# Segment attention on one core: where the same-segment products, the own values and the choice stand in the order of a step

## The chip, the cores and the metric

The kernel runs on one core of a Trainium2 chip. Each core has TensorE (PE in the rows, its weight loads PEld), VectorE (DVE), ScalarE (ACT), GpSimd (POOL), SyncE for DMAs (SP), a 128-partition SBUF and eight PSUM banks of 512 float32 columns per partition. The engines run their own instruction queues in order and wait for each other by semaphores. The metric is the time of one execution on the device in microseconds, as a median over runs; all data are float32 unless a row says otherwise.

## The reference, cut to what matters

Five layers, each added to the running activations `x` (32 x 32 tokens of 256 features): an attention with distance bias over a context, an attention over the 32 tokens of a batch, a quantised feed-forward layer, an attention over the context without heads, then the segment attention that the change touches, and a layer of experts. The segment attention is, with the layer norm of `x` as its input (16 heads of 16 features):

```python
long_out = _mha(x, lt_w_in, lt_b_in, lt_w_out, lt_b_out, H)
seg = jnp.argmax(x @ protos.T, axis=-1)
same = seg[:, :, None] == seg[:, None, :]
short_out = _mha(x, st_w_in, st_b_in, st_w_out, st_b_out, H, mask=same)
cnt = jnp.sum(jax.nn.one_hot(seg, NSEG, dtype=jnp.int32), axis=1)
tok_cnt = jnp.take_along_axis(cnt, seg, axis=1)
short_out = jnp.where((tok_cnt == 1)[..., None], x, short_out)
combined = jnp.concatenate([long_out, short_out], axis=-1)
return combined @ fus_w.T + fus_b
```

A token that is alone in its segment keeps its own features in place of the short output. `_mha` projects to queries, keys and values, takes the softmax of the scaled scores (with -1e9 where the mask is off) and weighs the values. The experts' layer routes each token to two of eight experts.

## The kernel before, in words

The 1024 tokens are eight tiles `t` of 128 tokens, each of four batches of 32. The segment attention (class `SegmentAttention`) works in steps `u = 2t + s`: an even step (`s = 0`) is the long attention of tile `t`, an odd step (`s = 1`) the short one. The steps are a pipeline written out by hand: in one step each engine does pieces of several tiles, in a fixed order, by the functions `pe_step`, `act_step`, `pool_step` and `dve_step`. Steps -3 to -1 run at the end of the stage before, 0 to 8 in a block of their own, 9 to 14 together with the first work of the experts' layer (`experts`), whose own order for the end of the last tiles follows the loop.

In step `u` PE does, in this order: in an odd step the transposes of the normalised tokens of tile t + 2 (`turn_tokens`) and of the one-hot segment of tile t + 1 (L2122), in an even step the segment logits of tile t + 1 (L2127); queries and keys of step u + 2 (`project_qk`, L859); the scores of step u + 1 (`per_batch`, L899), and at once the projection of its own values (`project_tokens`, L868); in an odd step the same-segment products of tile t + 1 (L2139), four of 8 x 32 by 8 x 32 which give 1 where two tokens of a batch share a segment; the weighing of the values of step u (`weigh_values`, L926); then in an even step the short output of tile t - 1 (`last_y`, L2169 and L2174), in an odd step the fused output of tile t - 1 (`fused_near` and `fused_far`, L2181 and L2187).

ACT copies what PE leaves: transposed tokens (L2062) and one-hot (L2065), keys (L2073) and queries (L2078) with their bias, the own values (L2028), the attention sums and each head's own part of the weighed values (L2033, L2036), then the exponent of step u + 1 (L2043), and in an even step the short output of tile t - 1 (L2049). POOL spreads the keys over heads (L875) and the values over batches (L882), adds a bias row (L2018) and takes the root for the normalisation (L1993).

DVE does in step `u`: `features` of step u - 1 (reciprocal of the sums, L2208, product, L2209, and a transpose of 32 x 32 blocks, L959), the transpose of the probabilities of step u (L936), in an even step the argmax of tile t + 1 (L2220 to L2227) and statistics of tile t + 3 (L2193 to L2196), in an odd step the normalisation of tile t + 3 (L2202), then `off_maximum` of step u + 1: in an odd step the maximum of the long scores and its subtraction (L2239, L2240), in an even step the mask, the maximum and the subtraction for the short ones (L2246, L2250, L2251). In an odd step follows the mask's making: a copy of the same-segment products out of PSUM (L2302), the mask (L2304) and the count of others in the segment (L2305, L2306). Last come, in an even step, the choice between short output and own features of tile t - 1 (`short`, L2262), in an odd step the add of the fused output to `x` (L2268).

One PSUM bank, `v_bank`, holds in turn the logits, the transposed one-hot, the own values and the same-segment products. Their uses are numbered in `v_use`; `vb_full` counts what PE has filled, `vb_done` what has been read, and PE waits before each use for the one before it to be read. The scores stand in banks 2 and 3, 256 columns in each; the columns behind are not used. PE raises `s_full` when the scores of a step are there, and DVE raises `s_read` when it has read them. `same_ready` tells that the mask is made, `short_ready` that the choice of a tile is done; PE's fused output and its next short output wait for it.

Of the kernel before, what the change touches and what calls it, by code (L numbers as in the profile page):

```python
# [25 lines left out]
NB, SQ, D, SK = 32, 32, 256, 257  # L26
NH, DH = 16, 16
P = 128
# [948 lines left out]
def there(u, count=NT):  # L977
    return not isinstance(u, int) or 0 <= u < count
# [944 lines left out]
class SegmentAttention:  # L1923


    def __init__(self, nc, in_wn, in_shared, sem, psum, bank, c, x, w, loaded):
# [29 lines left out]
        x_part, fused = f_bank[:, D:2 * D], f_bank[:, 0:D]  # L1956
        v_part, same_part = v_bank[:, 0:D], v_bank[:, D:D + SQ]
        logits, hot_part = v_bank[:, D + SQ:D + SQ + NE], v_bank[0:NE, D + SQ + NE:D + SQ + NE + P]
        y_part, others_part = y_bank[:, 0:D], y_bank[:, D:D + P]
# [7 lines left out]
        y_full, y_ready, short_ready = sem("y_full"), sem("y_ready"), sem("short_ready")  # L1967
        hot_ready, same_ready = sem("hot_ready"), sem("same_ready")
        qk_full, k_ready, q_ready, kbd_ready = sem("qk_full"), sem("k_ready"), sem("q_ready"), sem("kbd_ready")
# [6 lines left out]
        for u in range(-3, U + 2):  # L1976
# [7 lines left out]
            if there(u + 1, U):  # L1984
                v_use["v", u + 1] = len(v_use) + 1
            if s == 1 and there(t + 1):
                v_use["same", t + 1] = len(v_use) + 1
        self.ahead = in_shared.at
# [123 lines left out]
        def pe_step(pe, u):  # L2112
# [21 lines left out]
            if there(u + 1, U):  # L2134
                scores(pe, u + 1)
            if s == 1 and there(t + 1):
                pe.wait_ge(vb_done, v_use["same", t + 1] - 1)
                for b in range(BT):
                    ins = nc.tensor.matmul(same_part[SQ * b:SQ * b + SQ, :], hotT[:, SQ * b:SQ * b + SQ],  # L2139
                                           hotT[:, SQ * b:SQ * b + SQ], start=True, stop=True,  # L2140
                                           skip_group_check=True)
                ins.then_inc(vb_full, 1)
            if there(u, U):
                values(pe, u)
            if s == 0 and there(t - 1):
                last_y(pe, t - 1)
# [5 lines left out]
        def scores(pe, n):  # L2152
            pe.wait_ge(kbd_ready, n + 1)
            pe.wait_ge(q_ready, n + 1)
            at_least(pe, s_read, n)
            per_batch(nc, s_banks, tokens(qT[n % 2]), heads_apart(kbd[n % 2]), 0, True).then_inc(s_full, 1)
            at_least(pe, vb_done, v_use["v", n] - 1)
            project_tokens(nc, v_part, xT[:, n // 2], w[kinds[n % 2] + "_qkv"][:, :, 2 * D:3 * D]) \
                .then_inc(vb_full, 1)
# [69 lines left out]
        def off_maximum(dve, n):  # L2229
# [7 lines left out]
            at_least(dve, p_ready, n - 1)  # L2237
            if n % 2 == 0:
                st.link(dve, nc.vector.tensor_reduce(by_bank, banks, AX.X, ALU.max))  # L2239
                nc.vector.tensor_tensor(here[:].rearrange(in_banks_of, f=2), banks,  # L2240
# [43 lines left out]
        def dve_step(dve, u):  # L2284
# [3 lines left out]
            if there(u, U):  # L2288
                turn(dve, u)
            if s == 0 and there(t + 1):  # L2290
                argmax(dve, t + 1)
# [6 lines left out]
            if s == 1 and there(t + 1):  # L2298
                n = t + 1
                dve.wait_ge(vb_full, v_use["same", n])  # L2300
                at_least(dve, y_full, n - 2)
                nc.vector.tensor_copy(same[:], same_part).then_inc(vb_done, 1)  # L2302
                dve.wait_ge(vb_done, v_use["same", n])
                st.done(nc.vector.tensor_scalar(shut[:], same[:], 1.0, 1e9, ALU.subtract, ALU.mult))  # L2304
# [4 lines left out]
                dve.sem_inc(same_ready, 1)  # L2309
            if s == 0 and there(t - 1):  # L2310
                short(dve, t - 1)
            if s == 1 and there(t - 1):
# [656 lines left out]
```

## Time and profile before

| what | value |
|---|---|
| median of 3 runs | 713.54 us (711.33 to 713.84) |
| profiled execution | 710.97 us, its span 709.2 us |
| PE busy | 626.6 us, 88% of the span |
| DVE busy | 459.7 us, 65% |
| ACT busy | 368.5 us, 52% |
| POOL busy | 314.7 us, 44% |
| mean granted clock of PE | 0.95 |

The span runs from the first instruction to the last; the profiled execution's own time is 1.8 us longer. The segment attention's loop lies between 459 and 563 us of it. A busy share is an average over stages with different limits, so the shares above say little about one stage; the busy time by stretch and the timeline of one pair of steps do. In a row of a timeline, the bracket at the end is the time for which the engine sat idle before the instruction, and what released it. Matmul records come two to a float32 matmul; their ends are modelled.

### The profile page before, as it was taken

How to read it: one execution, taken by the hardware profiler on the slowest of the kernel's cores; microseconds unless marked ns; L12 is line 12 of the kernel's file. 1: busy time of each engine (PE TensorE's matmuls, PEld its weight loads, DVE VectorE, ACT ScalarE, POOL GpSimd, SP SyncE). 2: the span in 40 equal slices, each digit the busy share in tenths (PEclk: the TensorE clock that was granted, in tenths of full speed). 3: DMA queues.
4: the chain of work that ended last, by engine and by line, in shares of the span. 5: the costliest groups of instructions: out<-in, count | busy, mean ns of one | idle time of the engine just before them, and what ended most of it. 6: DMA issues, size and time to landing. Idle time of an engine off the chain costs nothing.

```text
span 709.2 us, 18761 instructions
## 1 busy us (share of the span) xinstructions
PE 626.6 (88%) x7075; PEld 476.2 (67%) x7075; DVE 459.7 (65%) x1279; ACT 368.5 (52%) x992; POOL 314.7 (44%) x458
## 2 busy tenths in 40 slices
PE   4999999999999999779957999889998859999990
PEld 3788888888877787544445876668777645777760
DVE  1797777776686988843988735487888873333320
ACT  1656665656566897653956434356656521322220
POOL 1346666666653897300000302166655413655641
PEclk9999999999999999879977999999999978999995
DMA  8733333333300000291003347093020031444434
GB/s 276 260 100 91 83 73 89 88 87 74 86 2 4 3 4 4 96 352 59 0 0 144 120 158 293 2 394 128 3 68 2 2 114 45 63 66 68 62 39 73
DMA packets 31704, 65.20 MB, mean 92 GB/s; under 512 B 5792, under 2 KB 21792, under 8 KB 29312
## 3 DMA queue, kind: packets, MB, share of 16 engines
q1 hardware_dynamic: 26016, 55.73, 23.8%
q0 software_dynamic: 4688, 7.18, 6.4%
q8 instruction: 58, 0.95, 0.5%
q10 hardware_dynamic: 912, 1.10, 0.5%
q14 instruction: 30, 0.25, 0.1%
HBM read 57.67 MB, written 7.37 MB: 92 GB/s over the span
## 4 chain that ended last, share of the span: by engine, by line
PE 64%; DVE 21%; ACT 5%; issue 4%; DMA 2%; SPq 2%; POOL 1%; DVEq 0%; ACTq 0%; POOLq 0%
PE psum L2647 8%; PE psum L491 7%; PE psum L499 7%; PE psum L2657 4%; PE psum L529 4%; PE psum L1502 3%; PE psum L1479 3%; PE psum L859 3%; DVE ff_peak L1520 2%; PE psum L515 2%; PE psum L544 2%; PE psum L851 2%; PE psum L868 2%; PE psum L899 2%; DMA wn<-in_w_down 2%
## 5 line engine op out<-in xcount | busy, mean ns | idle before, releaser
L802 POOL TENSOR_SCALAR bias<-dist,cst 128x257 f32<-128x257 f32 x128 | 61.4, 499 | 74.1 <-issue 42.8
L491 PE MATMUL psum<-ctxT,shared 128*128 128x257 f32 x256 | 65.9, 401 | 2.3 <-DMA msk<-in_mask 2.2
L424 ACT ACTIVATE prob<-s_sb,negm 128x257 f32<-128x257 f32 x128 | 64.9, 509 | 1.4 <-DVE negm L665 1.3
L499 PE MATMUL psum<-shared,ctxT 128*128 128x256 f32 x256 | 60.6, 379 | 0.0
L661 DVE CUSTOM_DVE_ANT_0 s_sb<-psum,bias 128x257 f32<-128x257 f32 x128 | 46.6, 420 | 19.8 <-PE psum L515 17.2
L2647 PE MATMUL psum<-ex_w,shared 128*128 x184 | 58.3, 460 | 0.6 <-ACT shared L2540 0.6
L1741 POOL TENSOR_TENSOR wn<-wn,cst 128x1 f32<-128x1 f32 x8 | 4.7, 590 | 120.8 <-DVE wn L1868 120.8
L491 PEld LDWEIGHTS psum<-ctxT,shared 128*128 128x128 f32 x256 | 47.1, 194 | 12.6 <-issue 4.9
L413 ACT COPY kT<-psum 128x257 f32<-128x257 f32 x64 | 24.0, 375 | 60.3 <-PE psum L491 60.3
L499 PEld LDWEIGHTS psum<-shared,ctxT 128*128 128x128 f32 x256 | 46.2, 190 | 5.0
L2830 DVE TENSOR_TENSOR shared<-psum,shared 128x352 f32<-128x352 f32 x23 | 12.1, 525 | 48.6 <-ACT shared L2556 48.6
L2647 PEld LDWEIGHTS psum<-ex_w,shared 128*128 128x128 f32 x184 | 33.1, 190 | 15.4 <-issue 0.8
L1479 PE MATMUL psum<-shared,ff_used_up 128*128 128x512 f32 x96 | 41.6, 593 | 0.0
L875 POOL TENSOR_TENSOR shared<-shared,cst 128x512 f32<-128x512 f32 x32 | 35.1, 1117 | 7.7 <-ACT shared L2073 6.8
L2556 ACT ACTIVATE shared<-psum 128x352 f32<-128x352 f32 x23 | 10.7, 464 | 52.8 <-PE psum L2647 52.8
L2657 PE MATMUL psum<-ex_w,shared 128*128 x138 | 33.7, 380 | 0.8 <-DVE shared L2821 0.8
L681 DVE COPY pT<-psum 128x512 f32<-128x512 f32 x32 | 22.1, 691 | 17.9 <-PE psum L529 16.1
L529 PE MATMUL psum<-cst,prob 128*128 128x128 f32 x256 | 33.2, 273 | 0.2 <-DVE mx L661 0.2
L1479 PEld LDWEIGHTS psum<-shared,ff_used_up 128*128 128x128 f32 x96 | 18.1, 191 | 22.0 <-issue 21.5
L859 PE MATMUL psum<-shared,late 128*128 128x128 f32 x256 | 32.9, 283 | 0.0
L1520 DVE TENSOR_REDUCE ff_peak<-shared 128x1 f32<-128x512 f32 (+1 forms) x24 | 22.8, 952 | 14.6 <-ACT shared L1373 14.2
L529 PEld LDWEIGHTS psum<-cst,prob 128*128 128x128 f32 x256 | 29.5, 141 | 2.9 <-issue 0.4
(357 smaller groups left out, 1614.6 us busy)
## 6 DMA issues: line engine op xcount, KB each, us to landing
ctxT<-in_ctx_T SPq DMA_DIRECT2D x32, 257.0 KB
ex_w<-in_w SPq DMA_DIRECT2D x1, 5632.0 KB, 18.2
kpos<-in_kpos SPq DMA_DIRECT2D x32, 128.5 KB
msk<-in_mask SPq DMA_DIRECT2D x32, 128.5 KB
near_turned<-in_ctx_T_tiles SPq DMA_DIRECT2D x4, 1028.0 KB
ff_used_up<-in_ctx_T_tiles SPq DMA_DIRECT2D x4, 1028.0 KB
near_rows<-in_ctx_tiles SPq DMA_DIRECT2D x4, 1024.0 KB, 7.4
ff_used_up<-in_ctx_tiles SPq DMA_DIRECT2D x4, 1024.0 KB, 6.6
```

The costliest lines, as they stand in the source:

```text
L424: nc.scalar.activation(prob[n % 2][:, g, :], s_sb[n % 2][:, g, :], ACT.Exp, bias=negm[:, b, g:g + 1], accum_out=esum[t % 2][:, b, g:g + 1]) \
L491: ins = nc.tensor.matmul(kv[m][:, 0:SK], w["xa_k"][:, k, P * m:P * m + P], ctxT[n % BT][:, k, :], start=(k == 0), stop=(k == KT - 1))
L499: ins = nc.tensor.matmul(kv[0][:, D * i:D * i + D], ctxT[n % BT][:, k, P * i:P * i + P], w["xa_v"][:, k, :], start=(i == 0 and k == 0), st ...
L529: ins = nc.tensor.transpose(pt[j][:, at:at + P], prob[n % 2][:, g, P * i:P * i + P], c.ident)
L661: nc.vector.tensor_tensor_reduce(s_sb[n % 2][:, g, :], sc[g][:, 0:SK], bias[n % 2][:, g, :], 1.0, float("-inf"), ALU.add, ALU.max, mx[:, b ...
L802: nc.gpsimd.tensor_scalar(bias[n % 2][:, g, :], dist[n % 2][:], c.slope[:, g:g + 1], 1.0 / FAR, ALU.mult, ALU.mult).then_inc(bias_ready, 1)
L859: ins = nc.tensor.matmul(dst[:, P * m:P * m + P], weight[:, k, P * m:P * m + P], xT[:, k, :], start=(m == 0 and k == 0), stop=True, skip_g ...
L875: return eng.tensor_tensor(kbd, src.unsqueeze(2).broadcast_to([P, BT, 4, SQ]), head.unsqueeze(1).unsqueeze(3).broadcast_to([P, BT, 4, SQ]) ...
L1479: ins = nc.tensor.matmul(bank[2 + n % 6][:], wt[:, k, P * m:P * m + P], xT[:, k, 512 * h:512 * h + 512], start=(k == 0), stop=(k == KT - 1))
L1520: return nc.vector.tensor_reduce(peak[:, i, n:n + 1], piece, AX.XY if len(piece.shape) == 3 else AX.X, ALU.max, apply_absolute_value=True)
L2647: ins = nc.tensor.matmul(y_bank[part][:, 0:FE], rT[j % 2][:, k, :], ex.w1[:, bass.ds(e, 1), k, FE * part:FE * part + FE].rearrange("p a f ...
L2657: ins = nc.tensor.matmul(o_bank[j % 2][:, 0:D], gT[j % 2][0:n, ch, :], ex.w2[0:n, bass.ds(e, 1), ch, :].rearrange("p a d -> p (a d)"), sta ...
```

## The change

The same-segment products of a tile are written into bank 2 behind the score columns, in the function `scores`, right after the scores of the next long step and ahead of the signal for them. The own values are projected in a function of their own, which `pe_step` calls behind the weighing of the values. DVE copies the products out in `off_maximum`, ahead of the maximum, and raises a new semaphore, `same_taken`, for which the mask's making waits; the copy there and its numbered use of `v_bank` are gone. The choice of tile t - 1 stands in the odd step behind the transpose of the probabilities, where it stood at the end of the even step.

```diff
--- before.py
+++ after.py
@@ -1954,8 +1954,8 @@
         f_bank, v_bank, y_bank = bank[0], bank[1], bank[4]
         fold_bank, row_bank = bank[3], bank[4]
         x_part, fused = f_bank[:, D:2 * D], f_bank[:, 0:D]
-        v_part, same_part = v_bank[:, 0:D], v_bank[:, D:D + SQ]
-        logits, hot_part = v_bank[:, D + SQ:D + SQ + NE], v_bank[0:NE, D + SQ + NE:D + SQ + NE + P]
+        v_part, same_part = v_bank[:, 0:D], psum[:, 2, D:D + SQ]
+        logits, hot_part = v_bank[:, D:D + NE], v_bank[0:NE, D + NE:D + NE + P]
         y_part, others_part = y_bank[:, 0:D], y_bank[:, D:D + P]
 
         st = Steps(sem("dve_steps"))
@@ -1965,7 +1965,7 @@
         f_full, f_done = sem("f_full"), sem("f_done")
         vb_full, vb_done = sem("vb_full"), sem("vb_done")
         y_full, y_ready, short_ready = sem("y_full"), sem("y_ready"), sem("short_ready")
-        hot_ready, same_ready = sem("hot_ready"), sem("same_ready")
+        hot_ready, same_taken, same_ready = sem("hot_ready"), sem("same_taken"), sem("same_ready")
         qk_full, k_ready, q_ready, kbd_ready = sem("qk_full"), sem("k_ready"), sem("q_ready"), sem("kbd_ready")
         vbd_ready, s_full, s_read, sub_ready = sem("vbd_ready"), sem("s_full"), sem("s_read"), sem("sub_ready")
         p_ready, pT_ready = sem("p_ready"), sem("pT_ready")
@@ -1983,8 +1983,6 @@
                 v_use[("logits", "hot")[s], t + 1] = len(v_use) + 1
             if there(u + 1, U):
                 v_use["v", u + 1] = len(v_use) + 1
-            if s == 1 and there(t + 1):
-                v_use["same", t + 1] = len(v_use) + 1
         self.ahead = in_shared.at
         self.last_u = U + 2
 
@@ -2133,15 +2131,10 @@
                 project_qk(nc, qk_bank, w[kinds[s] + "_qkv"], xT[:, n // 2]).then_inc(qk_full, 1)
             if there(u + 1, U):
                 scores(pe, u + 1)
-            if s == 1 and there(t + 1):
-                pe.wait_ge(vb_done, v_use["same", t + 1] - 1)
-                for b in range(BT):
-                    ins = nc.tensor.matmul(same_part[SQ * b:SQ * b + SQ, :], hotT[:, SQ * b:SQ * b + SQ],
-                                           hotT[:, SQ * b:SQ * b + SQ], start=True, stop=True,
-                                           skip_group_check=True)
-                ins.then_inc(vb_full, 1)
             if there(u, U):
                 values(pe, u)
+            if there(u + 1, U):
+                own_values(pe, u + 1)
             if s == 0 and there(t - 1):
                 last_y(pe, t - 1)
             if s == 1 and there(t - 1):
@@ -2153,7 +2146,16 @@
             pe.wait_ge(kbd_ready, n + 1)
             pe.wait_ge(q_ready, n + 1)
             at_least(pe, s_read, n)
-            per_batch(nc, s_banks, tokens(qT[n % 2]), heads_apart(kbd[n % 2]), 0, True).then_inc(s_full, 1)
+            ins = per_batch(nc, s_banks, tokens(qT[n % 2]), heads_apart(kbd[n % 2]), 0, True)
+            if n % 2 == 0:
+                pe.wait_ge(vb_done, v_use["hot", n // 2])
+                for b in range(BT):
+                    mine = slice(SQ * b, SQ * b + SQ)
+                    ins = nc.tensor.matmul(same_part[mine, :], hotT[:, mine], hotT[:, mine], start=True, stop=True,
+                                           skip_group_check=True)
+            ins.then_inc(s_full, 1)
+
+        def own_values(pe, n):
             at_least(pe, vb_done, v_use["v", n] - 1)
             project_tokens(nc, v_part, xT[:, n // 2], w[kinds[n % 2] + "_qkv"][:, :, 2 * D:3 * D]) \
                 .then_inc(vb_full, 1)
@@ -2236,6 +2238,7 @@
             dve.wait_ge(s_full, n + 1)
             at_least(dve, p_ready, n - 1)
             if n % 2 == 0:
+                nc.vector.tensor_copy(same[:], same_part).then_inc(same_taken, 1)
                 st.link(dve, nc.vector.tensor_reduce(by_bank, banks, AX.X, ALU.max))
                 nc.vector.tensor_tensor(here[:].rearrange(in_banks_of, f=2), banks,
                                         by_bank.unsqueeze(3).broadcast_to(each), ALU.subtract) \
@@ -2287,6 +2290,8 @@
                 features(dve, u - 1)
             if there(u, U):
                 turn(dve, u)
+            if s == 1 and there(t - 1):
+                short(dve, t - 1)
             if s == 0 and there(t + 1):
                 argmax(dve, t + 1)
             if s == 0 and there(t + 3) and t + 3 >= 2:
@@ -2297,18 +2302,14 @@
                 off_maximum(dve, u + 1)
             if s == 1 and there(t + 1):
                 n = t + 1
-                dve.wait_ge(vb_full, v_use["same", n])
                 at_least(dve, y_full, n - 2)
-                nc.vector.tensor_copy(same[:], same_part).then_inc(vb_done, 1)
-                dve.wait_ge(vb_done, v_use["same", n])
+                dve.wait_ge(same_taken, n + 1)
                 st.done(nc.vector.tensor_scalar(shut[:], same[:], 1.0, 1e9, ALU.subtract, ALU.mult))
                 st.link(dve, nc.vector.tensor_tensor(same[:], same[:], c.eq, ALU.subtract))
                 st.link(dve, nc.vector.tensor_tensor(
                     others[n % 2][:], same[:].unsqueeze(1).broadcast_to([P, BT, SQ]),
                     c.row.unsqueeze(2).broadcast_to([P, BT, SQ]), ALU.mult))
                 dve.sem_inc(same_ready, 1)
-            if s == 0 and there(t - 1):
-                short(dve, t - 1)
             if s == 1 and there(t - 1):
                 add(dve, t - 1)
 
```

## Rows read from the trace of the kernel before

**Rows 1.** Busy time by stretch, three pairs of steps: length, each engine, clock, DMA.
```profile
489.12:502.42 13.30, 12.84 (x207) 10.96 (x206) 10.95 (x29) 8.28 (x26) 7.77 (x8) 1.00 0.01 4
...
528.78:543.40 14.62, 13.68 (x213) 11.66 (x212) 12.21 (x31) 8.22 (x26) 7.28 (x8) 1.00 0.01 3
543.40:558.20 14.80, 12.06 (x218) 9.10 (x216) 12.37 (x32) 8.33 (x26) 7.87 (x9) 1.00 0.01 3
```

**Rows 2.** DVE's waits, 475 to 560 us: total us, times, longest.
```profile
DVE shared L2262 <- ACT wn L2049: 9.2, 6, 2.2
```

**Rows 3.** PE's waits, 475 to 560 us.
```profile
PE psum L2139 <- ACT shared L2028: 2.8, 6, 0.5
PE psum L868 <- DVE shared L2221: 1.7, 2, 1.3
```

**Rows 4.** Busy time by stretch, from one weighing of values to the next.
```profile
492.32:498.76 6.44, 5.98 (x106) 5.07 (x105) 4.86 (x12) 4.99 (x16) 5.13 (x6) 1.00 0.01 4
498.76:505.62 6.86, 6.51 (x104) 5.46 (x96) 6.09 (x19) 3.29 (x10) 2.64 (x3) 1.00 0.01 4
```

**Rows 5.** Timeline, one pair of steps: start, length, engine, line, idle before.
```profile
490.22 0.67 DVE L936 STREAM_TRANSPOSE wn<-wn 128x512 f32<-128x512 f32 x1
...
492.32 0.70 PE L926 MATMUL psum<-shared,wn 64*64 64x66 f32 x32
492.43 0.37 ACT L2028 COPY shared<-psum 128x256 f32<-128x256 f32 x1 [0.51 <-PE psum L868]
...
492.95 0.49 PE L2169 MATMUL psum<-shared 128*128 128x128 f32 x2
493.09 0.17 ACT L2033 COPY shared<-psum 128x16 f32<-128x16 f32 x1 [0.28 <-PE psum L926]
493.16 1.49 ACT L2036 COPY wn<-psum 32x256 f32<-32x256 f32 x4
...
494.00 0.79 DVE L2251 TENSOR_TENSOR shared<-shared 128x512 f32<-128x512 f32 x1
...
494.88 0.63 ACT L2043 ACTIVATE wn<-shared 128x512 f32<-128x512 f32 x1 [0.24 <-DVEq L2253]
...
495.65 1.04 POOL L882 TENSOR_TENSOR shared<-shared,cst 128x512 f32<-128x512 f32 x1
...
496.19 0.46 DVE L2262 COPY_PREDICATED shared<-psum,wn 128x256 f32<-128x256 int32 x1 [1.41 <-ACT wn L2049]
496.30 0.25 ACT L2065 COPY shared<-psum 8x128 f32<-8x128 f32 x1
...
496.55 0.23 DVE L2208 RECIPROCAL shared<-shared 128x16 f32<-128x16 f32 x1
...
497.64 0.67 DVE L936 STREAM_TRANSPOSE wn<-wn 128x512 f32<-128x512 f32 x1
...
498.57 0.26 PE L2139 MATMUL psum<-shared 8*32 8x32 f32 x8 [0.46 <-ACT shared L2028]
...
500.36 1.03 PE L2187 MATMUL psum<-late,shared 128*128 128x256 f32 x4
...
502.08 0.42 DVE L2268 TENSOR_TENSOR x<-psum,x 128x256 f32<-128x256 f32 x1 [0.21 <-DVE shared L2306]
```

**Rows 6.** Timeline, the last step of the stage's loop.
```profile
556.78 1.13 PE L868 MATMUL psum<-late,shared 128*128 128x256 f32 x4
...
560.10 0.97 PE L926 MATMUL psum<-shared,wn 64*64 64x66 f32 x32 [2.19 <-DVE wn L936]
```

**Rows 7.** Busy time by stretch: the two low stretches of PE's clock.
```profile
474.00:476.00 2.00, 2.00 (x15) 2.00 (x16) 1.75 (x6) 1.10 (x3) 0.63 (x1) 0.76 0.86 369
...
560.00:562.00 2.00, 1.90 (x36) 1.78 (x37) 1.93 (x4) 0.85 (x4) 0.71 (x3) 0.59 0.00 0
```

**Rows 8.** Two DVE lines: count, ns min/median/max, first and last start.
```profile
L2202 DVE TENSOR_SCALAR shared<-x,shared x8: 374/822/1144, 440.8 to 524.7; 128x256 f32<-128x256 f32 x8
...
L2304 DVE TENSOR_SCALAR shared<-shared x8: 183/886/926, 462.1 to 555.3; 128x32 f32<-128x32 f32 x8
```

## The prediction

> **What bounds the kernel now.** I read the chain of waits first, for the place: in the segment stage it runs almost wholly through DVE, leaving it at one spot of every even step, the choice (L2262). Then the busy time by stretch, cut where DVE begins the features of an even step, so that one stretch is a pair of steps. A pair takes 13.30 us, of which DVE works 10.95 and PE 12.84; later pairs, into which the experts' normalisation is woven, take 14.62 and 14.80, with DVE at 12.21 and 12.37 [rows 1]. Neither engine is full. DVE's idle time is one wait: for ACT's copy of the short output before the choice, 9.2 us in six times, 2.2 the longest [rows 2], so about 1.4 in each of the others. PE's waits are for ACT's copy of the own values before the same-segment products, 2.8 us in six times, and for the argmax [rows 3].
>
> How near PE is to its limit is read from weighing to weighing: even to odd 6.44 us with 5.98 busy, odd to even 6.86 with 6.51 [rows 4]. A pair in which PE never waited would take 5.98 + 6.51 = 12.49. So about 0.8 us of 13.30 can go per pair, whatever DVE gains.
>
> **The change, part by part.** No instruction goes or comes; the order changes. V is the start of the weighing of values (L926).
>
> *The products.* The eight records of 0.26 us, 0.46 behind that wait in a steady pair [rows 5], move behind the scores, and the score signal comes 0.2 us later. PE no longer waits there for ACT's copy of the own values: 0.46 per odd step. In its place it waits for ACT's copy of the transposed one-hot, which today ends at 496.55 [rows 5]. Behind that wait stand the odd step's scores signal and everything PE does later. It is covered only if ACT is punctual, see below. DVE's copy of the products now precedes the maximum; its cost of 0.2 us stays. In the start-up step, where the products sat behind the projection, I take nothing: the copy and the products now stand ahead of the maximum and cost 0.2 + 0.2, about what DVE waits for them today. Bounds 0.5 either way.
>
> *The own values.* The projection (1.13 us, as in [rows 6]) moves from ahead of the weighing to behind it. PE's argmax wait goes, since the argmax now has the weighing to finish in. But ACT's copy of the own values, which today is done before the weighing ends, now stands between the weighing and ACT's reading of the attention sums, and POOL's spreading waits for it. Every ring of a step has to be walked again, from V, with lengths from [rows 5]:
>
> Own-value ring: weighing 0.63 (492.32 to 492.95), projection 1.13 + 0.04, copy 0.37, sums and own parts 1.56 (493.09 to 494.65), hand-over 0.05, so DVE's features start at V + 3.78 at the earliest. Features to transpose 1.09 (496.55 to 497.64), transpose 0.67 + 0.05: next weighing at V + 5.6.
> ACT ring: exponent at V + 3.8, from its start to the end of the one-hot copy 1.67 (494.88 to 496.55), products 0.26: V + 5.7.
> POOL ring of an even step: from DVE's transpose to the end of the spreading 6.47 (490.22 to 496.69). V is then 0.72 behind the transpose, so the next weighing can start at V + 5.8.
> DVE: transpose to the end of the masked subtraction 4.57 (490.22 to 494.79), hand-over 0.06, features 1.09, odd step from its transpose 4.78 (497.64 to the pair's end at 502.42), choice 0.46, features 1.10: 12.06 per pair.
> Odd step, fused part: today L2187 ends 2.63 behind V (498.76 to 501.39); 1.13 later that is 3.76, then add 0.34, features and transpose 1.82: V + 5.9.
>
> All of these stand below PE's 5.98 and 6.51, and DVE's 12.06 below 12.49, but by only 0.2 to 0.6. PE becomes the bound, with four others right beneath it. I take 12.6 per pair, a gain of 0.7; the ends are 0.9 and nothing.
>
> *The choice.* It moves behind the transpose of the odd step. Queued behind it on DVE are the normalisation, the maximum, and the add; PE's fused part waits for it, but at V + 1.7 of the odd step, when it is long done. The short output is copied by V + 5.2 (exponent at 3.8, two times 0.63 and a start), and DVE comes to the choice at V + 3.78 + 1.09 + 0.6 = 5.5. So this wait goes, and what is late next is PE.
>
> *The tail of the loop.* The last own-value projection today stands in a hole: it starts at 556.78, and PE then waits until 560.10, 2.19 us with nothing to do [rows 6]. From there the chain of waits is PE's, and its granted clock in the next 2 us is 0.59 of 2.4 GHz, most of them at its lower level of 1.2 [rows 7]. The projection moves into that stretch: at least 1.1 us, at most 1.13/0.59 plus ACT's copy 0.37, or 2.3. I take 1.5 lost, nearer the lower end since PE does other work there too.
>
> *What may meet elsewhere.* L2202 takes between 374 and 1144 ns and L2304 between 183 and 926 [rows 8], for the same shapes; the long ones lie beside POOL's instructions. Both stand in the odd step, in front of what DVE owes PE. Their medians, 822 and 886, say that they are mostly caught today; caught always, a pair's DVE work grows by at most 0.32 + 0.04, to 12.4, and freed it shrinks by up to 1.2. That decides only once PE is no longer the bound. The Trainium skill's page SBUF — State Buffer, section Who interferes with whom, has it that DVE and GpSimd share a port pair and whoever starts first holds it for the whole instruction. These rows agree; it speaks against shifting POOL's spreading later without a look at where DVE then stands.
>
> **The sum.** Three steady pairs: 3 x 0.7 = 2.1. Two pairs with experts' work, where DVE with 12.2 and 12.4 busy of 14.6 and 14.8 is the longer: the choice's wait, 2 x 1.4 = 2.8 (ends 0.9 and 1.9). The first pair with a choice, part of it at a lowered clock (0.76 at 474 us [rows 7]), where the wait is 2.2 but the later own-value copy takes its place for part: 1.2 (ends 0.7 and 2.2). Tail -1.5. Together 2.1 + 2.8 + 1.2 - 1.5 = 4.6 us less. The profiled execution took 710.97 us, 1.8 of it outside its span of 709.2, which would make it 706.4. The median of the runs shown is 2.6 above it, so the forecast is 713.54 - 4.6 = 708.9.
>
> **The rivals.**
> *More.* If the clock stays high at 474 us and every pair reaches 12.49: 3 x 0.8 + 3.8 + 2.2 - 1.1 = 7.3, or 706.2. For: PE's idle pieces get shorter. Against: PE's idle hole ahead of 560 us grows. Chance 0.12.
> *One wait for another.* DVE leaves the choice's wait only to wait at the features for ACT's sums, now at V + 3.78 where today the features start at V + 4.23. If V keeps its place, that is 0.45 per pair, and the choice's 0.46 comes back in the odd step: nothing in three pairs, 0.5 in the first, 0.9 in each of the two with experts' work, -1.5: 712.7. For: the margins of 0.2. Against: V itself moves up, since PE has 0.8 to give. Chance 0.23.
> *Slower, POOL's ring.* The even step's spreading ends at V + 5.8 where PE needs it at 5.98. From V + 6.44 on the step is longer than today. If the lock catches POOL's and DVE's pieces against each other once more (the 0.74 between the ends of L2304), it is 6.5, and with the odd step as today at 6.86 a pair takes 13.4; twice more, 14.1. Five pairs at 0.8 more and the tail 1.5 give 713.54 + 5.5 = 719.0. For: POOL starts behind DVE's statistics, which are now later against V. Against: it needs two catches in every pair. Chance 0.10.
> *The change does not do what it says:* the products wait for the one-hot copy as long as they did for the own values. The ACT ring gives V + 5.7, so they would need ACT to be 0.8 late; then steady pairs gain nothing and the rest stays: 1.2 + 2.8 - 1.5 = 2.5, or 711.0. It shares its chance with the second rival.
>
> **How the numbers follow.** The forecast has 0.55. A measurement of this kernel can tell 0.5% (3.6 us) from no change. The forecast's own spread, 2.5 to 6.5 us of gain, passes 3.6 in about eight of ten, 0.44; with the first rival that is 0.56 for faster. The rest of the forecast and the second rival make 0.34 for the same, the third 0.10 for slower. The range leaves out the slower rival and part of the first: 704.5 to 714.0, the upper end being no gain, within the spread of the three runs.
>
> **What would show it.** Steady pairs of 12.4 to 12.8 us from features to features, with PE busy above 95%; no wait at L2262 and none on ACT at L2139; ACT's copy of the own values right behind the weighing, DVE's features 3.8 us behind V. The stretch from the last even weighing to the router 1 to 2 us longer. Wrong if pairs stay at 13 us with a new wait at L2208 or at the weighing (then second or third rival), if the products wait on L2065, or if the clock falls in a new place.

## The result, and the profile after

The changed kernel takes 706.67 us (median of 6 runs, 705.57 to 708.65) beside 712.88 us for the kernel before (6 runs, 710.71 to 714.29): 6.2 us less between the medians. The ratio on record, which is estimated from the runs of both kernels and is not the quotient of the two medians, is 0.9923, 95% interval 0.9904 to 0.9943, so some 5.5 us less; the ratios further down are of the same kind. The profiled execution took 707.23 us, its span is 705.4 us, and the mean granted clock 0.949 against 0.950.

To see where the time went, the segment stage of both traces is cut at the same instructions: from the first argmax to the features of step 0, then from features to features (L2208, now L2210), and last from the features of step 14 to the router's first reduction. The cuts of [rows 1] lie 0.1 us ahead of the features in the experts' pairs, hence 14.71 and 14.79 here. Each column is one profiled execution. Times in us; the experiments' columns are used further down.

| part | before | changed | choice alone | products alone | products + choice |
|---|---|---|---|---|---|
| start-up | 14.27 | 13.74 | 14.25 | 13.51 | 13.50 |
| first step | 6.26 | 6.33 | 6.26 | 6.13 | 6.13 |
| first pair with a choice | 13.89 | 12.82 | 13.87 | 13.00 | 12.87 |
| steady pair 1 | 13.30 | 12.15 | 12.66 | 13.31 | 12.15 |
| steady pair 2 | 13.18 | 12.80 | 12.88 | 13.05 | 12.30 |
| steady pair 3 | 13.18 | 12.81 | 12.87 | 13.06 | 12.34 |
| experts' pair 1 | 14.71 | 13.59 | 13.94 | 14.86 | 13.41 |
| experts' pair 2 | 14.79 | 13.63 | 13.64 | 14.80 | 13.64 |
| tail, to the router | 17.38 | 18.45 | 17.08 | 17.09 | 17.38 |
| stage | 120.96 | 116.32 | 117.45 | 118.81 | 113.72 |

The stage is 4.64 us shorter; two more profiles of the changed kernel, below, have it 3.67 and 3.17 us shorter. The rest of the program, whose code is the same, ran 1.97 us longer ahead of the stage and 1.13 shorter in the experts' part. The start of the stage lies between 454.6 and 458.8 us in the profiles of all variants, and between 454.9 and 456.7 in three of the changed kernel itself, so these differences are the spread of an execution and not the change.

The busy time of the changed kernel, pair by pair, answers to [rows 1]. Columns: stretch, length, busy time of PE, PE's weight loads, DVE, ACT, POOL, granted clock, DMA share, GB/s.

```profile
489.56:501.71 12.15, 11.85 (x201) 10.40 (x200) 11.09 (x29) 7.90 (x26) 7.64 (x8) 1.00 0.01 3
501.71:514.51 12.80, 12.67 (x209) 11.34 (x209) 11.74 (x29) 8.08 (x27) 8.29 (x9) 1.00 0.01 3
514.51:527.32 12.81, 12.17 (x203) 10.71 (x203) 11.68 (x30) 7.99 (x26) 8.20 (x9) 1.00 0.28 93
527.32:540.91 13.59, 12.47 (x206) 11.01 (x206) 12.46 (x32) 7.99 (x26) 7.38 (x8) 1.00 0.01 3
```

By these columns PE looks full, 95 to 99% of a steady pair. DVE's and PE's waits from 475 to 560 us say otherwise; they answer to [rows 2, 3].

```profile
DVE shared L2210 <- ACT wn L2034: 1.2, 1, 1.2
DVE shared L2307 <- DVE shared L2243: 1.1, 5, 0.2
DVE x L2271 <- DVE shared L2309: 1.1, 5, 0.2
DVE x L2271 <- PE psum L2189: 1.0, 1, 1.0
```

```profile
PE psum L926 <- DVE wn L936: 6.6, 9, 2.7
```

The choice (L2265) is gone from DVE's list, and the two lines with 1.1 us in five times are DVE waiting for its own instruction just before, 0.2 us each. PE's waits for ACT's own values and for the argmax are gone too. What is new is that PE waits nine times for DVE's transpose before the weighing, three of them, 0.8 us together, in the steady pairs. The chain of work that ended last, followed back through the three steady pairs, settles it: it holds 32.8 us of DVE's instructions and none of PE's; what remains, some 5 us, is time for which the profile shows no engine. So DVE sets the length of a pair, and PE follows. The timeline of the first steady pair shows the new order and answers to [rows 5]: start, length, engine, line.

```profile
491.39 0.70 PE L926 MATMUL psum<-shared,wn 64*64 64x66 f32 x32
492.01 1.13 PE L868 MATMUL psum<-late,shared 128*128 128x256 f32 x4
493.18 0.37 ACT L2026 COPY shared<-psum 128x256 f32<-128x256 f32 x1 [1.20 <-PE psum L868]
493.51 1.49 ACT L2034 COPY wn<-psum 32x256 f32<-32x256 f32 x4
495.37 0.25 DVE L2210 RECIPROCAL shared<-shared 128x16 f32<-128x16 f32 x1
495.97 0.62 ACT L2047 ACTIVATE wn<-psum,shared 128x128 f32<-128x128 f32 x2
496.74 0.25 ACT L2063 COPY shared<-psum 8x128 f32<-8x128 f32 x1
496.81 0.67 DVE L936 STREAM_TRANSPOSE wn<-wn 128x512 f32<-128x512 f32 x1
497.04 0.15 PEld L2154 LDWEIGHTS psum<-shared 8*32 8x32 f32 x8 [0.34 <-ACT shared L2063]
497.40 0.42 DVE L2265 COPY_PREDICATED shared<-psum,wn 128x256 f32<-128x256 int32 x1
497.54 0.70 PE L926 MATMUL psum<-shared,wn 64*64 64x66 f32 x32 [0.23 <-DVE wn L936]
```

The own values' copy stands behind the weighing as foreseen, and ACT's own parts end at 495.00, 0.37 before DVE starts the features. The products start right after the one-hot copy, with 0.34 us of wait at their weight load. ACT's copy of the short output (L2047) ends at 496.59, 0.8 us before the choice.

Pairs of 12.15 and 12.80 us do the same work. They differ in three DVE instructions of the odd step. The first three rows are of the first steady pair, the others of the second:

```profile
497.71 0.40 DVE L2204 TENSOR_SCALAR shared<-x,shared 128x256 f32<-128x256 f32 x1
499.75 0.58 DVE L2307 TENSOR_SCALAR shared<-shared 128x32 f32<-128x32 f32 x1 [0.22 <-DVE shared L2243]
500.45 0.70 DVE L2309 TENSOR_TENSOR shared<-shared,cst 128x128 f32<-128x128 f32 x1
...
509.87 1.05 DVE L2204 TENSOR_SCALAR shared<-x,shared 128x256 f32<-128x256 f32 x1
512.56 0.98 DVE L2307 TENSOR_SCALAR shared<-shared 128x32 f32<-128x32 f32 x1 [0.22 <-DVE shared L2243]
513.67 0.29 DVE L2309 TENSOR_TENSOR shared<-shared,cst 128x128 f32<-128x128 f32 x1
```

0.65 + 0.40 - 0.41 = 0.64, against a difference of 0.65 between the pairs. POOL's timeline beside them, first pair and second:

```profile
498.25 2.04 POOL L875 TENSOR_TENSOR shared<-shared,cst 128x512 f32<-128x512 f32 x2 [0.95 <-ACT shared L2071]
500.25 0.76 POOL L2016 TENSOR_TENSOR x<-x,wn 128x256 f32<-128x256 f32 x1
...
509.73 2.08 POOL L875 TENSOR_TENSOR shared<-shared,cst 128x512 f32<-128x512 f32 x2 [0.27 <-ACT shared L2071]
511.78 0.72 POOL L2016 TENSOR_TENSOR x<-x,wn 128x256 f32<-128x256 f32 x1
512.46 1.03 POOL L882 TENSOR_TENSOR shared<-shared,cst 128x512 f32<-128x512 f32 x1
```

L2204 is short where it starts ahead of POOL's L875 (497.71 against 498.25) and long where it starts 0.14 us behind it (509.87 against 509.73). L2307 ends at 513.54 where POOL's L882 ends at 513.49. These are the catches of [rows 8]: a catch is a DVE instruction that takes longer because one of POOL's is running when it starts, and that ends about when POOL's does.

### The profile page after: what moved, and what is told of

Its sections match the earlier page's. It is cut to its first block, busy times and chain, and to the rows that moved or that the text cites. A ratio compares the mean times of both kernels' runs of the same rounds, so it can differ in the third digit from the quotient of the medians.

```text
span 705.4 us, 18761 instructions
## 1 busy us (share of the span) xinstructions
PE 621.6 (88%) x7075; PEld 476.0 (67%) x7075; DVE 460.2 (65%) x1279; ACT 366.2 (52%) x992; POOL 315.3 (45%) x458
## 4 chain that ended last, share of the span: by engine, by line
PE 64%; DVE 21%; ACT 3%; issue 3%; DMA 2%; SPq 2%; POOL 1%; DVEq 0%; ACTq 0%; POOLq 0%
PE psum L2648 8%; PE psum L491 7%; PE psum L499 7%; PE psum L2658 4%; PE psum L529 4%; PE psum L1502 3%; PE psum L1479 3%; PE psum L868 3%; DVE ff_peak L1520 2%; PE psum L515 2%; PE psum L544 2%; PE psum L859 2%; PE psum L851 2%; PE psum L899 2%; DMA wn<-in_w_down 2%
## 5 line engine op out<-in xcount | busy, mean ns | idle before, releaser
L875 POOL TENSOR_TENSOR shared<-shared,cst 128x512 f32<-128x512 f32 x32 | 35.1, 1116 | 6.9 <-ACT shared L2071 6.9
```

Of the source, the lines that this page charges most:

```text
L875: return eng.tensor_tensor(kbd, src.unsqueeze(2).broadcast_to([P, BT, 4, SQ]), head.unsqueeze(1).unsqueeze(3).broadcast_to([P, BT, 4, SQ]) ...
```

## The experiments

Diffs are against the changed kernel unless the text says otherwise. All leave the computation whole. "Stage" is the cut of the table above.

**The choice alone.** The kernel before, with only the choice moved.

```diff
+            if s == 1 and there(t - 1):
+                short(dve, t - 1)
             if s == 0 and there(t + 1):
                 argmax(dve, t + 1)
...
-            if s == 0 and there(t - 1):
-                short(dve, t - 1)
```

> The kernel before with the choice alone moved behind the odd step's transpose; products and own values stay where they were. Theory (DVE is the bound, its wait at the choice is what the change took away): the wait of 9.2 us at L2262 goes; PE keeps its 0.46 wait before the products, which holds a pair at about 12.49 + 0.5 = 13.0, so the three steady pairs give 0.2 to 0.3 each, the first pair 0.9, the two pairs with experts' work 1.1 each, the tail nothing: 3.5 to 4.2 us less than before, ratio 0.994 to 0.995. Rival (PE is the bound, the gain came from its own waits for ACT's copy and the argmax): steady pairs stay at 13.2, under 1 us in all, ratio 0.999.

Measured: 709.51 us, ratio 0.9951 (0.9930 to 0.9973); the stage 3.51 us shorter. The total is as expected, its parts are not: the steady pairs gave 1.25 together where 0.6 to 0.9 were expected, and the first pair 0.02 where 0.9 was. DVE's wait for the choice is gone there too, but PE runs at a granted clock of 0.80, 0.50 and 0.84 from 476 to 482 us. The largest wait of DVE and of PE in 475 to 560 us:

```profile
DVE x L2268 <- PE psum L2187: 3.7, 5, 1.2
```

```profile
PE psum L2139 <- ACT shared L2028: 2.8, 6, 0.5
```

Of the 9.2 us that DVE waited for the choice, 3.7 come back at the add, as a wait for PE's fused part, and PE keeps its 2.8 us ahead of the products. With the choice alone PE does become what DVE waits for: the chain through the three steady pairs holds 37.5 us of PE's instructions, 1.1 of ACT's and none of DVE's, where before it held 30.4 of DVE's and 1.8 of ACT's.

**PE's two moves without the choice.** The choice goes back to the end of the even step.

```diff
-            if s == 1 and there(t - 1):
-                short(dve, t - 1)
...
+            if s == 0 and there(t - 1):
+                short(dve, t - 1)
             if s == 1 and there(t - 1):
                 add(dve, t - 1)
```

> The changed kernel with the choice back at the end of the even step; products and own values stand in their new places. Theory (DVE's wait at the choice is the bound): the wait at the choice is back at 1.4 us or more in each pair, steady pairs 13.0 to 13.5, the last own-value projection still costs 1.1 in the tail: between the time before and 1.5 us above it, ratio 1.000 to 1.002. Rival (PE's own waits were the bound): steady pairs at 12.5 to 12.8, 4 us less, ratio 0.994.

Measured: 719.08 us, ratio 1.0099 (1.0078 to 1.0120): slower, by more than expected. The stage takes 127.51 us, with 18.02 in the first pair with experts' work. DVE's waits, and PE's clock in a part of that pair (columns as above):

```profile
DVE shared L2265 <- ACT wn L2047: 8.9, 6, 1.7
DVE x L2271 <- PE psum L2189: 6.8, 3, 4.4
```

```profile
544.00:546.00 2.00, 2.00 (x24) 1.61 (x17) 1.24 (x4) 0.00 (x0) 0.90 (x2) 0.50 0.00 0
```

The choice's wait stays nearly whole. PE, delayed by it, stood still for 2.23 us ahead of 543.33 us, and its clock then was 0.50, its lower level: 3.3 of the 6.6 us that the stage is longer than before lie in that pair. So the two moves on PE together cost time while the choice waits; what each does is seen in the next two experiments.

**The products alone.** The own values go back ahead of the weighing too, so that only the products' move is left.

```diff
+            if there(u + 1, U):
+                own_values(pe, u + 1)
             if there(u, U):
                 values(pe, u)
-            if there(u + 1, U):
-                own_values(pe, u + 1)
```

The choice stands at the end of the even step, as in the experiment ahead.

> The products' move alone: behind the scores, ahead of the own values, which stand ahead of the weighing as before; the choice at the end of the even step. Theory (DVE's wait at the choice bounds the kernel before, PE's wait at the products lies under it): the choice's wait stays at 1.4 us per pair, steady pairs 13.1 to 13.2, ratio 0.999 to 1.000. Rival (the products' wait is a limit of its own, as the 3.7 us suggest by which products and choice together beat the choice alone): steady pairs 12.8, ratio 0.995.

Measured: 710.55 us, ratio 0.9975 (0.9954 to 0.9995); the stage 2.15 us shorter. 0.76 of it is the start-up; 0.89 is the first pair with a choice, in which this execution has no low clock where the kernel before has 0.76 [rows 7]; the steady pairs have 0.24 together. So the theory holds for the steady pairs, and the time lies between what theory (0.999 to 1.000) and rival (0.995) had. There is no profile of the kernel before with the full clock in the first pair, so how much of the 0.89 is the move's is open. Against the experiment ahead, from which this one differs by the place of the own values alone, the stage is 8.7 us shorter, part of it through the low clock there. The choice's wait is still there:

```profile
DVE shared L2265 <- ACT wn L2047: 8.4, 6, 1.4
```

**Products and choice, own values as before.** The diff shown for the products alone; the choice stays where the change puts it.

> The changed kernel with the own-value projection back ahead of the weighing: products and choice in their new places. Theory (the choice's wait gives the gain, the products' move lifts PE's limit, and the own values' move is not needed): pairs as in the changed kernel, 12.2 to 12.8, but the tail keeps its hole, 1.1 us less than the changed kernel: 5.5 to 6 us under the time before, ratio 0.992. Rival (the own values' move is needed, since otherwise PE waits for the argmax and the features come too late): pairs at 12.9 to 13.1, ratio 0.995.

Measured: 705.35 us (6 runs, 702.52 to 706.58), ratio 0.9904 (0.9880 to 0.9928), better than expected; the stage 113.72 us, 2.6 us less than the changed kernel. The second steady pair, then DVE's first wait in the three:

```profile
501.82:514.12 12.30, 12.30 (x202) 10.49 (x202) 10.82 (x30) 8.34 (x26) 8.48 (x9) 1.00 0.02 3
```

```profile
DVE x L2271 <- PE psum L2189: 1.6, 3, 0.7
```

Here PE is busy without a gap and DVE waits for it. The chain through the three steady pairs holds 34.8 us of PE's instructions and 2.0 of DVE's: this version is the one that PE bounds, at 12.15, 12.30 and 12.34 us. DVE's L2204 and POOL's L875 in the second pair:

```profile
509.97 0.40 DVE L2204 TENSOR_SCALAR shared<-x,shared 128x256 f32<-128x256 f32 x1
...
512.00 0.29 DVE L2307 TENSOR_SCALAR shared<-shared 128x32 f32<-128x32 f32 x1 [0.21 <-DVE shared L2243]
```

```profile
510.07 2.18 POOL L875 TENSOR_TENSOR shared<-shared,cst 128x512 f32<-128x512 f32 x2 [0.51 <-ACT shared L2071]
```

L2204 starts 0.10 us ahead of L875 and keeps its 0.40, and L2307 is down from 0.98 to 0.29.

**The same pair of kernels again, on one chip**, since the two intervals overlap.

> The changed kernel with the own values ahead of the weighing, a second time, to set it beside the changed kernel on the same chip. Theory (the own values' move costs): stage of some 114 us against 116 to 117, the tail 17.1 to 17.5 against 18.4 to 19.4, so 1.5 to 2.5 us less than the changed kernel, 0.990 of the kernel before. Rival (the move costs only in the profile): the two times within 0.7 us.

> The changed kernel, unchanged, beside the run above on the same chip. Both theories: 0.9923 of the kernel before, within 0.002. By the theory it stands 1.5 to 2.5 us above the run with the own values ahead; by the rival within 0.7 us of it.

Measured: 705.98 us with the own values ahead (6 runs) and 708.18 us for the changed kernel (9 runs), ratios to the kernel before 0.9915 (0.9883 to 0.9946) and 0.9937 (0.9915 to 0.9959). The difference is 2.2 us, 95% interval by resampling the runs 0.1 to 4.5; over all runs of the two kernels (12 and 27, not all on one chip) it is 2.3 us, 0.5 to 3.4. The stages are 113.70 and 117.79 us. Both intervals leave out zero, but begin under the rival's 0.7 us; with the stages 4.1 us apart and the tails at 17.35 and 19.65, the theory is the likelier: the own values' move costs some 2 us, and the version without it has the lowest median of all that ran.

**The changed kernel a second time**, beside the products alone.

> The changed kernel again, unaltered, beside the other three on one chip. Expected 0.9923 as before, within 0.002. If the normalisation ahead of the choice (0.9957) is really slower, the changed kernel is lower than that by 0.003 here too; if that difference is the spread between executions, it lies at 0.994.

Measured: 707.35 us (12 runs), ratio 0.9925 (0.9905 to 0.9945). It repeats. By what was set down ahead of this run, that speaks for the normalisation ahead of the choice (0.9957, next) being slower than the changed kernel. All parts of the stage are as in the first profile within 0.02 us, but the tail is 19.38 us instead of 18.45.

**The normalisation ahead of the choice**, so that L2204 starts before POOL's L875.

```diff
+            if s == 1 and there(t + 3) and t + 3 >= 2:
+                norm_apply(dve, t + 3)
             if s == 1 and there(t - 1):
                 short(dve, t - 1)
...
-            if s == 1 and there(t + 3) and t + 3 >= 2:
-                norm_apply(dve, t + 3)
```

> The changed kernel with the normalisation of the odd step one place earlier on DVE, ahead of the choice. Theory (DVE is the bound after the change, and the difference between its steady pairs of 12.15 and of 12.80 is POOL catching L2204 and L2307): the normalisation starts 0.3 us earlier, ahead of POOL's spreading of the keys, takes 0.4 instead of 1.05, and all three steady pairs come near 12.2: 1 to 1.5 us less than the changed kernel, ratio to before 0.990. Rival (PE bounds the changed kernel at 12.5 and DVE has slack): no difference from the changed kernel, ratio 0.992.

Measured: 708.43 us (8 runs), ratio 0.9957 (0.9938 to 0.9977): missed. The second steady pair, DVE and then POOL:

```profile
507.33 0.38 DVE L2204 TENSOR_SCALAR shared<-x,shared 128x256 f32<-128x256 f32 x1
...
509.67 0.65 DVE L2307 TENSOR_SCALAR shared<-shared 128x32 f32<-128x32 f32 x1 [0.21 <-DVE shared L2243]
...
510.45 1.01 DVE L2309 TENSOR_TENSOR shared<-shared,cst 128x128 f32<-128x128 f32 x1
```

```profile
507.50 2.09 POOL L875 TENSOR_TENSOR shared<-shared,cst 128x512 f32<-128x512 f32 x2 [0.27 <-ACT shared L2071]
...
510.25 1.07 POOL L882 TENSOR_TENSOR shared<-shared,cst 128x512 f32<-128x512 f32 x1
```

The edit does to L2204 what it should (1.05 to 0.38), and L2307 falls by 0.33; but L2309 now starts 0.20 us behind L882 and pays 1.01 instead of 0.29. Net 0.28 per pair, 12.80 to 12.53: the catch has moved. That the pair follows DVE's instructions to 0.01 us shows again that DVE bounds it. The median is no better than the changed kernel's, and the ratio is above the changed kernel's 0.9923, 0.9925 and 0.9937: in this profile the stage is 116.29 us, since the first experts' pair takes 13.87 instead of 13.59 and the tail 18.94. The intervals overlap a little, so that the move costs time as a whole is likely, not shown; that it gains none is clear.

**Own values ahead and the normalisation first**, both edits together.

> Products and choice in their new places, own values ahead of the weighing as before, and the normalisation one place earlier on DVE, ahead of the choice. Theory (PE bounds the steady pairs at 12.3 once the own values are ahead, DVE's catches matter only in the pairs where L2204 was caught): the first two pairs with a choice lose 0.3 to 0.6, the rest as with the own values ahead, ratio 0.989 to 0.990. Rival (nothing is left on DVE): no difference, 0.9904.

Measured: 706.92 us (7 runs), ratio 0.9918 (0.9887 to 0.9948), the stage 114.18 us: not as expected, nothing gained over the own values ahead alone. The first pair with a choice lost 0.3 as foreseen (12.87 to 12.55), but the second and third steady pairs grew from 12.30 and 12.34 to 12.67 and 12.54. In the second:

```profile
512.85 0.74 DVE L2308 TENSOR_TENSOR shared<-shared,cst 128x32 f32<-128x32 f32 x1
...
513.62 1.06 DVE L2309 TENSOR_TENSOR shared<-shared,cst 128x128 f32<-128x128 f32 x1
```

POOL's L2016 started at 512.81 and its L882 at 513.49, just ahead of each. The catches have moved here too, DVE works 11.61 us of this pair instead of 10.82, and the chain is back on DVE: 32.3 us of its instructions in the three pairs and none of PE's, though PE's busy time is 12.67 of 12.67.

**Own values ahead in the last step alone**, for the tail.

```diff
+            if u == TAIL:
+                own_values(pe, u + 1)
             if there(u, U):
                 values(pe, u)
-            if there(u + 1, U):
+            if there(u + 1, U) and u != TAIL:
                 own_values(pe, u + 1)
```

> The changed kernel with the own-value projection ahead of the weighing in the last step of the loop alone. Theory (the projection stands in the way of a stretch that PE bounds, where before it lay in a hole): from the last even features to the router 17.3 to 17.5 us instead of 18.45, 1.0 us less than the changed kernel, pairs unchanged at 12.2 to 12.8. Rival (the tail is set by DVE and ACT, not by PE's order): 18.4 as in the changed kernel.

Measured: 706.98 us (8 runs), ratio 0.9924 (0.9897 to 0.9950). In the trace the tail falls to 17.08 us, a little below what was expected, and all other parts stay; in the times the difference is 0.4 us from the changed kernel on the same chip, within their spread.

## Why the prediction was right, and where it was not

**The total.** Forecast 4.6 us less. The stage of the first profile is 4.64 shorter, of the two later ones 3.67 and 3.17, and the three measurements of the changed kernel give 0.9923, 0.9925 and 0.9937, or 4.5 to 5.5 us. The forecast of 708.9 us lies 2.2 above the first median: 0.7 of that is the starting point, 713.54 where six runs gave 712.88. That the first profile agrees to 0.04 is luck: by part the forecast was 0.2 too high for the steady pairs, 0.5 for the experts' pairs and 0.1 for the first pair, and too low by 0.4 for the tail and 0.5 for the start-up.

**Start-up:** forecast 0 within 0.5; the trace has 0.53 less. The products alone give 0.76 less and the choice alone 0.02, so the saving comes with the products' move, which the prediction set off as equal.

**The choice:** its wait went, in every pair. Forecast for the first pair 1.2, measured 1.07; for the two with experts' work 2.8, measured 2.28. With the choice alone the stage gains 3.51, with the products alone 2.15, with both 7.24: neither carries the gain by itself, and each is worth more behind the other (the choice 5.1, the products 3.7). The first pair's part is not the choice's: alone it gained 0.02 there, the products alone 0.89. The low clock of [rows 7] goes along with it. It is there in the kernel before and with the choice alone, and from 474 to 482 us in none of the ten profiles in which the products are moved (one of them, the two moves on PE, has a low clock later in that pair, 488 to 492). That the products' move keeps the clock up is not shown by one profile each of the first two.

**The products:** PE's wait for the own values went, and no wait for the one-hot of more than the 0.34 at the weight load came, so "the products wait for the one-hot copy as long as they did for the own values" falls. Alone the move is worth 2.2 us of the stage, behind the choice 3.7 (117.45 to 113.72), of which 1.0 is the first pair, where the choice alone ran at the low clock, and 0.75 the start-up.

**The own values: the step that failed.** The prediction had "PE becomes the bound, with four others right beneath it", and therefore of L2202 and L2304: "That decides only once PE is no longer the bound." In the changed kernel DVE is the bound: PE waits nine times for its transpose, DVE waits for no other engine in a steady pair, and the chain through these pairs holds none of PE's instructions. The floor of 12.49 us was not one: a pair took 12.15, and 12.30 with PE busy throughout. It was the sum of busy times between waits [rows 4], and matmuls' ends are modelled. The same work shows 12.84 us of PE busy in the pair of [rows 1] and 11.85, 12.67 and 12.17 in the changed kernel, so such a sum is no measure of the time that PE needs. The nearest of the rings was DVE's, predicted at 12.06; it came out at 12.15, and at 12.80 where POOL catches L2204 and L2307. That is above the 12.4 which the prediction gave for "caught always": it added what is missing from the medians, 0.32 + 0.04, but the pair that the 12.06 was taken from had only 1.44 us for the two lines, as the next two rows show, and caught both they take 1.05 + 0.98 = 2.03.

```profile
498.23 0.59 DVE L2202 TENSOR_SCALAR shared<-x,shared 128x256 f32<-128x256 f32 x1
...
500.59 0.85 DVE L2304 TENSOR_SCALAR shared<-shared 128x32 f32<-128x32 f32 x1
```

The three steady pairs average 12.59 against the forecast 12.6: the size was met by luck, by another mechanism than the one named. With the own values ahead, L2204 starts just ahead of POOL's, the catches of L2204 and L2307 go, and PE does bound, at 12.3: that is 0.5 us in two pairs each that the move costs and the prediction did not price. What the move was to save, PE's wait for the argmax, did go, and it bought nothing: with the own values ahead that wait is 3.3 us in three times, and the stage is 2.6 us shorter all the same.

The Trainium skill's SBUF — State Buffer, Who interferes with whom, which lets the first of DVE and GpSimd to start hold the shared port pair, agrees with three of the four starts shown: 0.17 and 0.10 us ahead of L875 L2204 is short though the two overlap, 0.14 behind it is long. The fourth, 0.54 ahead, says nothing, since L2204 is over before L875 starts. What POOL pays for the overlap is small in these rows: L875 takes 2.09 and 2.18 us there and 2.04 and 2.08 in the changed kernel.

**The tail:** forecast 1.5 lost, ends 1.1 and 2.3; measured 1.07, and 2.0 and 2.3 in the other two profiles (19.38 and 19.65). The 1.07 sets a tail at the full clock beside one of the kernel before in which it was low [rows 7]. At the full clock the loss is 1.4 (18.45, of which 0.2 through a clock that falls in its last microsecond, against 17.08, 17.09 and 17.08 with the choice alone, the products alone and the own values ahead in the last step), at the low clock 2.0 and 2.3 (against 17.38). So the forecast holds better than the 1.07 says. With the own values ahead in the last step the loss is gone. The cause is the one given: the projection left a hole and stands in the chain. The low clock, where it falls, falls behind the same wait as before; that it might not fall was not foreseen.

**The signs.** Steady pairs of 12.4 to 12.8: 12.15 to 12.81. DVE's features 3.8 us behind V: 495.37 - 491.39 = 3.98, and DVE's own chain, not ACT, is what sets it. PE busy above 95%: true, and worthless as a sign, since PE was waiting for DVE at the same time.

**The rivals.** "One wait for another" falls: but for 0.16 us in the tail, the wait of the features for ACT's sums appears only in the stage's first two steps (1.2 us the longer). "Slower, POOL's ring" falls too, but its ingredient, catches between POOL and DVE, is what the own values' move pays with. "More" (706.2) named a clock that stays high at 474 us; it did, and the first pair still took 12.82, and the steady pairs averaged 12.59 and not 12.49. The first median, 706.67, lies nearer to its figure than to the forecast's 708.9; measured by the ratios, 4.5 to 5.5 us less, the gain is nearer to 4.6 than to its 7.3.

## What to carry to other kernels

Add up each engine's own chain, not its busy time: where PE's busy share is near 100%, ask the waits and the chain who is late before calling it the bound. When several moves come in one change, price each against the order the others leave: here the choice and the products gained 3.5 and 2.2 us of the stage alone and 7.2 together, and the own values' move cost 2.6 of that. A DVE instruction that started just behind one of POOL's cost 2.6 and 3.5 times its length (L2204 1.05 us against 0.40, L2309 1.01 against 0.29); moving one moved the catch to another in both experiments that tried it, so count the whole step and not the line.

## What the runs showed of the hardware

The granted clock after a wait of PE is not fixed by the kernel. In all three profiles of the changed kernel PE waits 2.67 us ahead of the last even weighing (L926). In the first the clock stays 1.00 (second row: 558 to 560); in the third it is 0.50, the lower level of 1.2 GHz, over the same work:

```profile
556.38 0.70 PE L926 MATMUL psum<-shared,wn 64*64 64x66 f32 x32 [2.67 <-DVE wn L936]
```

```profile
558.00:560.00 2.00, 2.00 (x19) 1.88 (x17) 1.42 (x5) 1.78 (x6) 1.38 (x3) 1.00 0.00 0
```

```profile
555.26 1.16 PE L926 MATMUL psum<-shared,wn 64*64 64x66 f32 x32 [2.67 <-DVE wn L936]
```

```profile
557.00:559.00 2.00, 2.00 (x8) 1.73 (x7) 1.31 (x5) 0.55 (x3) 0.10 (x1) 0.50 0.00 0
```

The weighing takes 1.16 us there instead of 0.70, and the tail 19.65 instead of 18.45. Nor is it one length of wait: with the products alone the same weighing came after a wait of 2.20 us and the clock stayed at 1.00, in the kernel before after 2.19 us and it fell [rows 6, 7]. What decides is open.
